# Two residual layers on eight images: the second residual add moved from VectorE into an accumulating DMA

## What is computed

```
x1  = x  + L0(gn(x))     # 1x1 convs to q, k, v; rotary on q, k; linear attention over 4096 tokens; 1x1 conv with bias
out = x1 + L1(gn(x1))    # 1x1 conv (w_in); 8x8 patch FFT, filter, inverse; 3x3 depthwise conv;
                         # gelu(first half) * second half; 1x1 conv (w_out), no bias
```

## Time and profile before

| | |
|---|---|
| Time, median of 3 runs | 4020.65 us (4017.44 to 4023.14) |
| Span of the profiled execution, first to last instruction | 4023.8 us |
| Busy: PE, DVE, ACT, POOL | 90%, 85%, 34%, 36% |
| One step of part C with all its work (steps 3 to 6) | 22.3 us |
| Period of one image | about 495 us |

### The profile page before, as it was taken

One profiled execution on the slowest core, in us unless ns is written; L12 is line 12 of the kernel. 1 busy time (PEld: TensorE's weight loads), 2 busy tenths in 40 slices (PEclk: granted clock), 3 DMA queues, 4 the chain that ended last, 5 costly groups with the idle time before them and its releaser, 6 DMA issues.

```text
span 4023.8 us, 60589 instructions
## 1 busy us (share of the span) xinstructions
PE 3617.9 (90%) x17488; PEld 2941.8 (73%) x17488; DVE 3421.6 (85%) x5124; ACT 1368.3 (34%) x2293; POOL 1436.5 (36%) x793
## 2 busy tenths in 40 slices
PE   5988999889998899988999889997899979999898
PEld 5976679666796667966589665896659966598665
DVE  7987999779897798977989779897798878988788
ACT  2323434234332343423433233331433314333142
POOL 2542235421354123551235411454115442155411
PEclk9999999899998999989999899998999989999899
DMA  5213231233212232123221323213222132221422
GB/s 198 71 57 125 94 111 55 71 110 109 96 55 86 102 110 88 63 86 110 94 103 47 107 90 110 88 47 121 85 100 88 55 126 87 94 95 39 141 71 102
DMA packets 186256, 370.98 MB, mean 92 GB/s; under 512 B 7946, under 2 KB 9010, under 8 KB 185778
## 3 DMA queue, kind: packets, MB, share of 16 engines
q1 hardware_dynamic: 186034, 368.26, 26.6%
HBM read 267.56 MB, written 100.66 MB: 92 GB/s over the span
## 4 chain that ended last, share of the span: by engine, by line
issue 54%; POOL 22%; PE 12%; DVE 8%; ACT 2%; POOLq 1%; DMA 1%; DVEq 0%; ACTq 0%; SPq 0%
POOL x_lo L415 11%; POOL t L422 9%; POOL qn L459 2%; PE bank L1058 2%; DVE nrm L793 2%; PE bank L1078 2%; PE bank L1079 2%; DVE qt_lo L808 2%; PE bank L1083 1%; PE bank L967 1%; DVE bn_x L854 1%; ACT qt_hi L552 1%; DVE acc L888 1%; PE bank L1127 0%; POOL qn L452 0%
## 5 line engine op out<-in xcount | busy, mean ns | idle before, releaser
L415 POOL TENSOR_TENSOR x_lo<-xa,x_hi 128x512 fp32r<-128x512 f32 x363 | 547.2, 1522 | 1493.5 <-ACT x_hi L504 1493.5
L888 DVE SCALAR_TENSOR_TENSOR acc<-big,wdw,acc 128x512 f32<-128x512 f32 x1280 | 955.6, 808 | 15.9 <-ACT big L566 13.5
L980 PE MATMUL bank<-w_lo,x_hi 128*128 128x384 f32 x2322 | 795.5, 343 | 10.7 <-issue 10.7
L979 PE MATMUL bank<-w_hi,x_hi 128*128 128x384 f32 x2322 | 794.0, 342 | 4.0 <-ACT x_hi L504 4.0
L422 POOL TENSOR_TENSOR t<-t 128x768 f32<-128x768 f32 x256 | 534.1, 2087 | 731.6 <-DVE t L729 731.5
L984 PE MATMUL bank<-w_hi,x_lo 128*128 128x384 f32 x2322 | 543.9, 342 | 0.5 <-POOL x_lo L415 0.5
L739 DVE SCALAR_TENSOR_TENSOR kt<-t 128x384 f32<-128x384 f32 x256 | 530.7, 2073 | 0.0
L509 ACT ACTIVATE t<-t 128x768 f32<-128x768 f32 x256 | 217.3, 849 | 874.5 <-POOL t L422 874.5
L980 PEld LDWEIGHTS bank<-w_lo,x_hi 128*128 128x128 f32 x2322 | 444.4, 191 | 13.0 <-issue 13.0
L979 PEld LDWEIGHTS bank<-w_hi,x_hi 128*128 128x128 f32 x2322 | 445.8, 192 | 6.3 <-ACT x_hi L504 4.4
L984 PEld LDWEIGHTS bank<-w_hi,x_lo 128*128 128x128 f32 x2322 | 424.7, 191 | 1.4 <-POOL x_lo L415 1.4
(11 more groups left out here) (112 smaller groups left out, 6235.0 us busy)
## 6 DMA issues: line engine op xcount, KB each, us to landing
xr<-x SPq DMA_DIRECT2D x128, 768.0 KB, 4.7
xa<-x SPq DMA_DIRECT2D x66, 768.0 KB, 5.9
x_scratch<-xr SPq DMA_DIRECT2D x64, 768.0 KB, 3.5
xa<-x_scratch SPq DMA_DIRECT2D x64, 768.0 KB, 5.8
xr<-x_scratch SPq DMA_DIRECT2D x64, 768.0 KB, 4.7
out<-xr SPq DMA_DIRECT2D x64, 768.0 KB, 3.5
big<-x SPq DMA_DIRECT2D x8, 768.0 KB, 9.9
w_raw<-wqkv_t SPq DMA_DIRECT2D x1, 1728.0 KB, 7.0
```

What stands on the lines that cost most here:

```text
L415: nc.gpsimd.tensor_tensor(dst, src, hi, ALU.subtract).then_inc(s_lo, 1)
L888: nc.vector.scalar_tensor_tensor(dst, src, wdw[:, k, q:q + 1], so_far, ALU.mult, ALU.add)\
L979: nc.tensor.matmul(dst, hi(k), whi(k), start=first and k == 0, stop=False)
L980: nc.tensor.matmul(dst, hi(k), wlo(k), start=False, stop=False)
```

## The change

The tensor for x1 in DRAM (`x1_scratch`) is gone: part B stores x1 in `out` itself, and part C loads `xa` from there. SP no longer loads x1 into `xr` in part C, and no longer stores `out` there. DVE no longer has the second residual. In its place ACT copies the three blocks of the last product from PSUM into `xr` (`evacuate`), and POOL issues a DMA that adds `xr` to `out` in DRAM (`add_to_out`, `accum_op=ALU.add`). Its end is counted by a new semaphore pair, `s_fin`: ACT waits on it before it writes the same half of `xr` again, two steps later, and SP at the end of each image, before it loads the next `x` into `xr`.

```diff
 # SP, part C
-                    if within(edge, 0, NCH, -2):
-                        wait(s_res, (i * 16 + c + NCH) * 3 + 3)
-                        sp.dma_start(chunk_of(out_v, i, c - 2), xr[:, par]).then_inc(s_st[par], 16)
-                    if within(edge, 0, NCH):
-                        wait(s_st[par], (i * 8 + h + 5) * 16)
-                        sp.dma_start(xr[:, par], chunk_of(x1_v, i, c)).then_inc(s_xr[par], 16)
-                steps(sp, NCH + 2, 2, NCH - 2, part_c)
+                steps(sp, NCH, 0, NCH - 2, part_c)
+                for par in range(2):
+                    wait(s_fin[par], (i * 4 + 4) * 16)
 # POOL, part C
+                def add_to_out(c, par):
+                    gp.wait_ge(s_res, (i * 16 + c + (NCH + 2)) * 3 + 3)
+                    gp.sem_inc(s_past, 1)
+                    gp.dma_start(chunk_of(out_v, i, c), xr[:, par], accum_op=ALU.add).then_inc(s_fin[par], 16)
+
                 def part_c(c, h, edge, par):
-                    for k in range(KB):
-                        low_part(i * 16 + c + (NCH + 1), k, 1 - par, patches=True)
-                steps(gp, NCH - 1, 0, NCH - 2, part_c)
-                for k in range(KB):
-                    low_part(i * 16 + 16, k, 0)
+                    if within(edge, 0, NCH):
+                        for k in range(KB):
+                            low_part(i * 16 + c + (NCH + 1), k, 1 - par, patches=(edge != NCH - 1))
+                    if within(edge, 0, NCH, -2):
+                        add_to_out(c - 2, par)
+                steps(gp, NCH + 2, 2, NCH - 2, part_c)
 # ACT, part C
+                def evacuate(c, h, edge, par, m, tail=None):
+                    r = i * 16 + c + NCH
+                    act.wait_ge(s_out, r * 3 + (m + 7))
+                    if m == 0:
+                        act.wait_ge(s_st[par], (i * 4 + 5) * 16)
+                        if edge not in (2, 3):
+                            act.wait_ge(s_fin[par], (i * 4 + h - 1) * 16)
+                    nc.scalar.activation(xr[:, par, m], bank[out_bank(m, tail)][:, :], ACT.Copy).then_inc(s_res, 1)
...
                         copy_t(T + 2, 0)
                         copy_img(T, c, 0)
+                    if gated:
+                        evacuate(c - 2, h, edge, par, 0, tail)
+                    if tile:
                         copy_t(T + 3, 1)
...
                             high_part(i * 16 + c + (NCH + 1), 1 - par, patches=True)
                         if edge == NCH - 1:
                             high_part(i * 16 + 16, 0)
+                    if gated:
+                        evacuate(c - 2, h, edge, par, 1, tail)
+                    if tile:
                         copy_img(T + 2, c, 2)
                         copy_img(T + 3, c, 3)
+                    if gated:
+                        evacuate(c - 2, h, edge, par, 2, tail)
...
-                steps(act, NCH + 2, 2, NCH - 2, part_c)
+                steps(act, NCH + 2, 4, NCH - 2, part_c)
 # DVE, part C
-                    if within(edge, 0, NCH, -2):
-                        residual(i * 16 + c + (NCH - 2), i * 12 + 8 + h, par, False, 0 if edge == NCH else 3 if edge == NCH + 1 else None,
-                                 (0, 1) if conv else (0, 1, 2))
                     if conv:
                         if tile:
                             dve.wait_ge(s_img, T + 6)
                         depthwise(c - 1, ND - 3 * KB, ND)
-                        if within(edge, 0, NCH, -2):
-                            residual(i * 16 + c + (NCH - 2), i * 12 + 8 + h, par, False, 0 if edge == NCH else None, (2,))
```

More of the change, by code:

```diff
@@ L119, in build_program @@
     out_v = out.rearrange("b (k p) (c n) -> b p k c n", p=P, n=CHUNK)
-    x1_dram = nc.dram_tensor("x1_scratch", (images, C, NTOK), fp32, kind="Internal").ap()
-    x1_v = x1_dram.rearrange("b (k p) (c n) -> b p k c n", p=P, n=CHUNK)
     ctx = ExitStack()
@@ L220, in build_program @@
         s_st = [sem(f"s_st{j}") for j in range(2)]
+        s_fin = [sem(f"s_fin{j}") for j in range(2)]
         s_stat = sem("s_stat")
@@ L342, in load_next @@
                     wait(s_stat, i * 8 + c + (NCH - 1))
-                    wait(s_st[par], (i * 8 + 1) * 16)
+                    wait(s_st[par], (i * 4 + 1) * 16)
                     sp.dma_start(xr[:, par], chunk_of(x_v, (i + 1) & (images - 1), c)).then_inc(s_xr[par], 16)
@@ L357, in part_b @@
                         wait(s_res, (i * 16 + c) * 3 + 3)
-                        sp.dma_start(chunk_of(x1_v, i, c - 2), xr[:, par]).then_inc(s_st[par], 16)
+                        sp.dma_start(chunk_of(out_v, i, c - 2), xr[:, par]).then_inc(s_st[par], 16)
                     if within(edge, 0, NCH):
                         wait(s_x1s, i * 8 + c + 1)
-                        wait(s_st[par], (i * 8 + h + 1) * 16)
+                        wait(s_st[par], (i * 4 + h + 1) * 16)
                         if edge in (0, 1):
@@ L371, in load_c @@
                     wait(s_lo, (i * 16 + c + NCH) * 3 + 3)
-                    wait(s_st[par], (i * 8 + h + 2) * 16)
-                    sp.dma_start(xa[:, par], chunk_of(x1_v, i, c)).then_inc(s_xa[par], 16)
+                    wait(s_st[par], (i * 4 + h + 2) * 16)
+                    sp.dma_start(xa[:, par], chunk_of(out_v, i, c)).then_inc(s_xa[par], 16)
                 for u in range(2):
@@ L385, in part_c @@
                             .then_inc(s_xa[par], 16)
-                    if within(edge, 0, NCH, -2):
-                        wait(s_res, (i * 16 + c + NCH) * 3 + 3)
-                        sp.dma_start(chunk_of(out_v, i, c - 2), xr[:, par]).then_inc(s_st[par], 16)
-                    if within(edge, 0, NCH):
-                        wait(s_st[par], (i * 8 + h + 5) * 16)
-                        sp.dma_start(xr[:, par], chunk_of(x1_v, i, c)).then_inc(s_xr[par], 16)
-                steps(sp, NCH + 2, 2, NCH - 2, part_c)
+                steps(sp, NCH, 0, NCH - 2, part_c)
+                for par in range(2):
+                    wait(s_fin[par], (i * 4 + 4) * 16)
             for par in range(2):
                 wait(s_xa[par], (images * 8 + 1) * 16)
-                wait(s_st[par], (images * 8 + 1) * 16)
+                wait(s_st[par], (images * 4 + 1) * 16)
+                wait(s_fin[par], images * 4 * 16)
         @block.gpsimd
@@ L594, in part_c @@
                     tile, conv, gated = (within(edge, 0, NCH, -d) for d in range(3))
+                    tail = None if tile else 3 * (c - NCH)
                     if tile:
@@ L757, in part_a @@
                             if j == 1:
-                                dve.wait_ge(s_xr[par], (i * 12 + 1 + h) * 16)
+                                dve.wait_ge(s_xr[par], (i * 8 + 1 + h) * 16)
                             ins = nc.vector.bn_stats(bn_x[:, j - 1, ds(c, 1), :].rearrange("p c s -> p (c s)"), xr[:, par, j - 1])
@@ L809, in low_q, with residual @@
                                                 ALU.subtract).then_inc(s_ql, 1)
-                def residual(r, loads, par, bias, tail=None, blocks=(0, 1, 2)):
+                def residual(r, loads, par, blocks=(0, 1, 2)):
                     dve.wait_ge(s_xr[par], loads * 16)
@@ L815, in residual @@
                         dve.wait_ge(s_out, r * 3 + (m + 7))
[L816 to L822, removed]
+                        nc.vector.scalar_tensor_tensor(xr[:, par, m], bank[2 + 3 * par + m][:, :], bfc_c[:, m:m + 1],
+                                                       xr[:, par, m], ALU.add, ALU.add).then_inc(s_res, 1)
                 dve.wait_ge(s_ka, i * 5 + 1)
@@ L841, in part_b @@
                         for m in range(KB):
-                            residual(i * 16 + c - 1, i * 12 + 4 + h + par, 1 - par, True, blocks=(m,))
+                            residual(i * 16 + c - 1, i * 8 + 4 + h + par, 1 - par, blocks=(m,))
                             dve.wait_ge(s_res, (i * 16 + c) * 3 + (m + 4))
@@ L847, in part_b @@
                     if within(edge, 0, NCH, -1):
-                        residual(i * 16 + c - 1, i * 12 + 4 + h + par, 1 - par, True)
+                        residual(i * 16 + c - 1, i * 8 + 4 + h + par, 1 - par)
                     if within(edge, 0, NCH, 1):
```

## The result

The changed kernel takes 4056.7 us (median of 4 runs, 4055.06 to 4061.85); the kernel before, beside it, 4019.6. The ratio is 1.0093 (95% interval 1.0078 to 1.0107): 37 us slower. The prediction was 4019, no change, with a range of 3994 to 4052. It was wrong: the kernel got slower. The profiled executions stand 29.6 us apart (4053.4 and 4023.8).

A forecast was written before the change was run, and what follows sets the result against it. PE was taken to bound the full step; on the profiled span 4023.8 + 7 (ACT copies) - 8 (changes of image) - 0.5 (end) = 4022.3, about 4019 us for the median, range 3994 to 4052.

The forecast's parts named there:

- The three last blocks run from 1533.2 to 1539.45 instead: Change of image: without its 2.81 us wait, PE runs chunk 7's last three blocks five us earlier.
- Tile 2 with its low clock: Change of image, after PE's restart: 5.8 us of work plus 2.1 us lost to the low clock after 7 us idle.
- Full steps: Part C: PE bounds, DVE's relief is worth nothing, and ACT's copy of block 1 costs 0.17 us a step, +7 us.
- Rival 4: Part C: DVE bounds after all, full steps give back 37 us and image changes 35, total 3950; chance 0.04.
- POOL's issue and the landing: Accumulating DMA at the change of image: issue 1.2 us, landing 7 us, of which 1.0 us is lost.
- the forecast's 4012 form: Landing in 3.8 to 5.6 us, so the 1.0 us per image change isn't lost: 4012 us; chance 0.07.
- Restart: Change of image: PE restarts at 1546.5, once `vt` is copied behind POOL's DMA issue, loop turn and rotated add.
- D and L: POOL at the change of image: DMA issue (D) taken as 1.2 us, turn of the loop (L) as 1.8 us.
- Rival 1: Change of image: POOL's issue is short, exp waits for ACT's chain alone, 27 us gained, total 3998; chance 0.18.
- Rival 2: Change of image: accumulating DMA lands late, in 12 us, total 4054, or 4081 with 15.8 us; chance 0.20.
- Rival 3: POOL's DMA issue is held by DVE's normalise of the next chunk, or takes 3 us: 4029 to 4034; chance 0.08.
- The end: End of the program: last copy 5 us earlier, last DMA 1.2 + 7 instead of about 4 us: -0.5 us.

The follow-up runs named there:

- the fill: Changed kernel plus four dummy float32 products of 384 columns on PE in the wait for chunk 7's gate: 4021.4 us, ratio 0.9996.
- one dummy: Changed kernel plus a single dummy product of 384 columns, in place of four, before the last three blocks: 4051.3 us, ratio 1.0088.
- the same fill: Kernel before plus four dummy products in PE's 2.81 us wait for the residual in the last steps: 4007.3 us, ratio 0.9969.
- the split wait with the fill: Changed kernel with four dummy products, and SP waiting for each half of `xr` just before loading it: 4011.8 us, ratio 0.9974.
- the plain DMA: Changed kernel with POOL's accumulating DMA made a plain store, so x1 is not added: 4045.2 us, ratio 1.0056.
- the early tile: Changed kernel with the next image's tile 0 (POOL rotated sum, ACT exp and `vt`) ahead of chunk 7's copies: 4077.5 us, ratio 1.0140.
- the split wait: Changed kernel, but SP waits for each half of `xr` to land just before loading it, not for both first: 4052.8 us, ratio 1.0073.
- with the split wait it gained 35: Changed kernel with the next image's tile 0 moved early and SP's landing wait made per half, no dummies: 4021.4 us, ratio 1.0004.
- another order on ACT: Changed kernel with four dummies, per-half landing wait, early tile 0, and ACT's copy of the first last block before it: 3996.8 us; without that reorder 4022.0 us.

## Why the prediction was wrong

**The step that failed.** "The three last blocks run from 1533.2 to 1539.45 instead. Five us are won at that point." They start 2.98 us after PE is ready, not 0.9, at the low clock, and take 11.4 us. The prediction charged the low clock behind the later idle (2.1 us) and not here. For an idle of 0.9 that was sound, since the clock is 1.00 with a gap of 0.78 in every step; the wait was sized wrong, and with it the clock behind it. The rows already held the price of the wait that came: the earlier trace rows has an idle of 2.81 followed by 1.54 for a first block, and the earlier trace rows 0.60 after 2.08.

Why 2.98? Two parts. First, I counted PE's readiness from rows of the kernel before in which the clock was itself low. These are its PE rows in step 7, from the inverse of tile 3 on:

```profile
1507.72 1.55 PE L1111 MATMUL bank<-t_mats,gb 128*128 128x128 f32 x6 [2.31 <-DVE gb L866]
1509.06 1.91 PE L1126 MATMUL bank<-gel,wout 128*128 128x512 f32 x2
1510.90 1.29 PE L1127 MATMUL bank<-gel,wout 64*128 64x512 f32 x2
```

and the same three after:

```profile
1517.16 0.94 PE L1123 MATMUL bank<-t_mats,gb 128*128 128x128 f32 x6 [1.73 <-DVE gb L883]
1517.93 1.02 PE L1138 MATMUL bank<-gel,wout 128*128 128x512 f32 x2
1518.89 1.12 PE L1139 MATMUL bank<-gel,wout 64*128 64x512 f32 x2
```

With less on DVE the gap shrank from 2.31 to 1.73 and the clock stayed up, in all eight images; behind the 2.31 it had fallen in seven of eight. From this inverse to the first block of chunk 6 PE now takes 1528.58 - 1517.16 = 11.42 us instead of 13.04 (1520.76 - 1507.72): 1.6 earlier. Second, the gate is 25.85 us behind the inverse where I had 25.4, since the residuals gave DVE 2.6 us there and not 3.1. DVE's gate in this image ends at 1541.60 + 1.41 = 1543.01:

```profile
1541.60 1.41 DVE L914 TENSOR_TENSOR gel<-gel,acc 128x512 f32<-128x512 f32 x2
```

0.9 + 1.6 + 0.45 = 2.95.

That the clock is the cause is shown: the fill brought 35 to 38 of the 37 us back, one dummy didn't, and the kernel before gained from the same fill at its own wait.

**Point by point**, in us for a change of image:

| Term | predicted | in the trace |
|---|---|---|
| Gate behind the inverse of step 7's tile 3 | 25.4 | 25.85 |
| Start of the last blocks to the end of ACT's last copy | 7.0 | 12.15 |
| From there to PE's restart | 6.3 | 5.2 |
| Tile 2 with its low clock | 7.9 | 7.4 |
| Tile 3 with what the landing costs | 6.8 | 7.9 |
| From the inverse to tile 4, against before | -1.2 | +4.0 (1575.87 - 1517.16 = 58.71 against 1562.44 - 1507.72 = 54.72) |

The rows of the table differ by +0.45, +5.15, -1.1, -0.5 and +1.1, together +5.1: this takes -1.2 to +3.9. So one term was missing. The others are each within about 1 us, and it is partly luck that they leave the sum alone: +1.55 and -1.6 cancel. The whole span follows: from image to image the last blocks start 498.7 us apart on the mean (498.0 to 500.0; 498.70 = 1543.16 - 1044.46 here) where it was 494.9 (494.3 to 495.1) before. The 3.9 between them are 4.0 from the table and 0.45 from the steps, less 0.6 of wait ahead of step 7's inverse; 3.9 x 7 = 27, and 2.5 more come from the ends of the program.

- *Full steps*: PE bounds them and DVE's relief is worth nothing there. Right: 0.09 a step where I took 0.17, the copy and the image copy overlapping more. Rival 4 is out.
- *POOL's issue and the landing*: 1.29 and 7.6 us, taken as 1.2 and 7 without a row. The landing cost 1.1 to 1.4 us (by the split wait with the fill), in place of 1.0. The estimate by the Trainium skill (DMA: Bandwidth & Descriptors, Anatomy of one DMA), 3.8 us, is for a plain copy; the plain DMA landed in 4.7, and the accumulating one is above both it and the 5.6 for doubled bytes. Of the forecast's 4012 form nothing is left.
- *Restart*: PE waits 5.86 for `vt`, behind POOL's issue and rotated sum, right in kind but narrowly. POOL starts the sum 0.82 us behind the start of the issue (1556.02 and 1556.84), where D and L, issue and turn of the loop, were taken as 3.0 together; the start of the issue is 0.7 behind ACT's last copy and not 0.1, and the sum takes 2.29 and not 1.8. So the restart comes 1.1 earlier. ACT's own chain, Rival 1's condition, ends only 0.37 us ahead of POOL's, so the restart is within 0.4 us of that rival's; the early tile takes the wait away.

```profile
1554.71 0.60 ACT L597 ACTIVATE xr<-bank 128x512 f32<-128x512 f32 x1 [3.41 <-PE bank L1139]
1557.51 1.28 ACT L512 ACT_TABLE_LOAD   x1 [2.21 <-issue]
1559.16 0.84 ACT L512 ACTIVATE t<-t 128x768 f32<-128x768 f32 x1 [0.37 <-POOL t L418]
```

- *Rival 2*, 4054, comes nearest in time but not in cause: it asks for a landing of 12 us.
- *Rival 3*, POOL against DVE: the 64 issues take 1267 to 1427 ns, with no long ones; it isn't seen. DVE's normalise, which it put beside the last issue, starts at 1546.66, 9 us ahead of it, so the case it named didn't arise here.
- *The end*: from the last image's first last block to the end it is 16.7 us and was 11.0. 2.0 of that is how late PE was before, and the gate now comes 2.6 earlier, so about 1 us is lost where I had 0.5 won; the last image's blocks aren't slowed in this execution.

With the fill the changed kernel takes 4021, the time that the prediction gave. The fill removes the one term that was missing, and the sum of the others comes out, with the cancelling just named.

## What to carry to other kernels

An engine that gets ahead of the next bound gains nothing and may lose: before you count a removed wait as won, find the wait that takes its place and see what PE's granted clock does behind one of that length in the trace you have. When you carry PE times from one place to another, carry the clock of the row too; a row at the low clock isn't the work's price. And take parallel waits together: the early tile alone cost about 20 us, with the split wait it gained 35, and with the fill it needed another order on ACT to gain anything.

## What the runs showed of the hardware that was not expected

- The same wait of 2.98 us for the gate brought a granted clock of 0.51 to 0.56 in seven images, and 1.00 in the last, where the blocks behind it took 6.4 us. It isn't the last image as such: with the plain DMA the fifth is spared, with the early tile the first, with one dummy (a wait of 2.25) the seventh, and with the split wait none; in the kernel before, the clock fell behind the 2.31 us of step 7 in all images but the second. So neither the length of the idle alone nor the place in the program decides; what does wasn't tried and is open.
- The clock doesn't fall at once: behind 2.26 us of idle the first pair ran at full speed and the second took 1.51 before the low clock's 2.07.
- An accumulating DMA of 768 KB from SBUF used about twice the packets of a plain one (25600 against 13312 for 64 of them), took 7.9% of the engines' time against 3.1%, 7.6 us to land against 4.7, and 0.5 us more of POOL for its issue.
